# Rebuilding the opening of an expert-mixing stage, with weight tiles of the next stage transferred earlier

## The chip, the cores and the metric

One Trainium2 chip, one core, one launch. The metric is the device time of the whole program in microseconds (us). Each run gives one time; a separate profiled execution gives the trace from which all rows below are taken. PE is the matrix engine (PEld its weight loads), DVE the vector engine, ACT the scalar engine, POOL GpSimd, SP the engine that issues the transfers here.

## The reference, cut to what matters

Eight blocks run one after the other on 1024 tokens of 512 features, each as `x = layernorm(x + block(x))`. The change touches the seams of four of them:

```python
x = _layernorm(x + _L0_attn_ref(x, ...))  # series + SwiGLU (F = 1248)
x = _layernorm(x + _L0_ffn_ref(x, ...))   # mix of 8 low-rank experts
x = _layernorm(x + _L1_attn_ref(x, ...))  # as laid out here: one key, so values only
x = _layernorm(x + _L1_ffn_ref(x, ...))   # SwiGLU, int weights with zeros and scales
...                                       # L2: convolution stack, two low-rank layers
x = _layernorm(x + _L3_attn_ref(x, ...))  # causal attention
x = _layernorm(x + _L3_ffn_ref(x, ...))   # SwiGLU, int weights with one scale each

def _L0_ffn_ref(x, W_org, lora_down, lora_up, lora_keys, Wq):
    base = jnp.einsum('bsi,oi->bso', x, W_org)
    q = jnp.einsum('bi,ki->bk', x.mean(axis=1), Wq)
    scores = jnp.einsum('bk,ek->be', q, lora_keys) / math.sqrt(K)
    coeffs = jax.nn.softmax(scores, axis=-1)
    h = jnp.einsum('bsi,eir->bser', x, lora_down)
    delta = jnp.einsum('be,bser,ero->bso', coeffs, h, lora_up)
    return base + delta
```

The expert mix is one weight matrix for all tokens, because the batch is one and the coefficients come from the mean token: `w_eff = W_org + down @ (coeff * up)`. So nothing of this block can start before the last token of the block ahead is normalised, summed, and taken through the query, the scores, the softmax and the scaled `up` matrix.

## The kernel before, in words

Tokens lie twice in SBUF: `x_tok` (tokens on partitions, 8 tiles of 128) and `x_feat` (features on partitions, 4 chunks of 128). Every engine has its own program; they meet through semaphores, and each stage is a `Block`, at whose end all engines wait for each other. There is no planner in the stages that the change touches; the order within an engine is the order of the code, except in the attention stage, where a list of events gives it.

A `Tail` ends each block of the model, tile by tile: DVE adds the product to `x_tok` (L95), takes statistics (L101, L102), ACT takes the root (L111), DVE normalises (L104, L105), PE transposes (L147), ACT copies the transposed tile to `x_feat` (L119). Where `start` is given, the copy goes straight into the next SwiGLU's input instead, split into a high part by ACT and a low part by DVE (`dve_low`, L125).

The first block is `swiglu` with a series added (`gradient_ffn`). In its second half, for each of eight token tiles, PE makes the series products (L820, from `series_part`, which ACT and DVE split at L799 and L811) and the down products (L577), and the tail follows one tile behind.

The expert stage is `lora_then_single_key`. Its opening: SP issues the transfers of the query matrix, the keys, `up` and `down`, then of `wo` (eight groups through three buffers, a buffer being free once `paired`), of `W_org` and of `wv`. DVE and ACT sum `x_feat` over the tokens (L1101, L1064), PE makes the query (L1019) and the scores (L1023), DVE and ACT the softmax (L1109 to L1114), ACT scales one half of `up`'s partitions and DVE the other, four instructions each (L1072, L1118). Then PE makes `delta`, 16 matrix products of four bytes a value (L1029, two records each), DVE adds `W_org` (L1137), and PE goes through the eight token tiles (L938). Merging `wv` and `wo` into `w_values` (L1042) and a second pass through the tiles (L938 again) follow. In that second pass the first two weight tiles of the next SwiGLU are already dequantised by DVE (`dequantise`: L325 takes the zeros off, L328 and L330 multiply by the scales), split by ACT (L364) and DVE (L369), and multiplied (L382).

The next stage, the SwiGLU with zeros and scales, has 14 weight tiles through two slots of `stage`, and one buffer each for zeros (`z_int`) and scales (`s_all`). SP loads tile f when tile f-2 is split (`w_lo`) and its zeros and scales when those of tile f-1 are used (`zs_used`). PE makes 48 products per tile (L560), ACT the silu (L614, L619), DVE the multiplication (L708, L715). POOL computes a table of rotations beside it (`Rotation.pool`), with instructions that get longer level by level.

## Time and profile before

| | us |
|---|---|
| runs | 1326.65, 1332.54, 1592.5 (median 1332.54) |
| profiled execution, time | 1336.08 |
| its span in the trace | 1334.4 |
| PE busy | 1244.7 (93% of the span) |
| DVE busy | 713.8 (53%) |
| ACT busy | 433.5 (32%) |
| POOL busy | 160.9 (12%) |
| mean granted PE clock | 0.971 of full |

The profiled execution's time exceeds its span by 1.7 us, which lie around the program. Engines work at the same time, so their busy times don't add up; what counts is the chain of waits, and on a kernel with PE at 93% that is first of all where PE stands still.

### The profile page before, as it was taken

The page shows a single profiled execution, that of the slowest core. Times are in us where ns is not written, and L with a number is a line of the kernel's source. Part 1 is how long each engine was busy: PE and PEld are TensorE (multiplying, and loading weights), DVE is VectorE, ACT ScalarE, POOL GpSimd, SP SyncE. Part 2 cuts the span into 40 slices and gives each one's busy share as a digit, 9 for nine tenths or more (in the row PEclk, how much of TensorE's full clock was granted, in tenths as well). Part 3 has the DMA queues.
Part 4 walks back from the last instruction along what each step waited for, and adds up shares of the span by engine and source line. Part 5 has one row for each costly group of instructions (what it writes and reads, how often), then busy time and mean ns, then how long its engine had stood idle before and what let it go on. Part 6 is the DMA issues. An engine that isn't in the chain of part 4 may idle for free. (4 is left out here: it accounts for less than half of the span.)

```text
span 1334.4 us, 14306 instructions
## 1 busy us (share of the span) xinstructions
PE 1244.7 (93%) x5325; PEld 845.4 (63%) x5336; DVE 713.8 (53%) x1191; ACT 433.5 (32%) x743; POOL 160.9 (12%) x214
## 2 busy tenths in 40 slices
PE   7899999699988999999887988899999998999998
PEld 4788688344477788788654435455555543688886
DVE  4421534368737655553434749787776744344344
ACT  2121422211111113321233221265666567222221
POOL 0000000000057300101111250000011124000000
PEclk9899999799999999998898989999999999999999
DMA  8110000643044562103000010000000000122001
GB/s 338 32 48 16 0 1 0 250 169 141 1 166 178 195 229 83 45 0 133 2 0 1 0 48 1 1 1 2 2 1 1 3 3 0 48 95 71 0 25 40
DMA packets 18264, 79.06 MB, mean 59 GB/s; under 512 B 3104, under 2 KB 3872, under 8 KB 16032
## 3 DMA queue, kind: packets, MB, share of 16 engines
q1 hardware_dynamic: 18208, 78.32, 16.1%
q8 instruction: 34, 0.56, 0.2%
q14 instruction: 22, 0.18, 0.0%
HBM read 75.95 MB, written 2.10 MB: 58 GB/s over the span
## 5 line engine op out<-in xcount | busy, mean ns | idle before, releaser
L2264 DVE TENSOR_REDUCE mqa_top<-psum 128x1 f32<-128x512 f32 (+3 forms) x304 | 186.3, 656 | 48.1 <-PE psum L2056 25.7
L2171 ACT ACTIVATE mqa_prob<-psum 128x512 f32<-128x512 f32 x288 | 156.5, 603 | 81.2 <-PE psum L2086 77.6
L560 PE MATMUL psum<-L_ffn_x,L_ffn_w_up 128*128 128x512 f32 x624 | 146.3, 396 | 8.7 <-DVE L_ffn_hidden L708 4.8
L560 PEld LDWEIGHTS psum<-L_ffn_x,L_ffn_w_up 128*128 128x128 f32 x624 | 118.9, 191 | 36.1 <-DVE L_ffn_hidden L708 6.3
L560 PE MATMUL psum<-L_attn_x,L_attn_w_up 128*128 128x512 f32 x456 | 106.2, 395 | 3.9 <-DVE L_attn_hidden L708 3.9
L560 PEld LDWEIGHTS psum<-L_attn_x,L_attn_w_up 128*128 128x128 f32 x456 | 87.2, 192 | 22.6 <-issue 4.3
L2086 PE MATMUL psum<-mqa_stack_back,mqa_keys 100*128 100x512 f32 x208 | 95.5, 459 | 0.9 <-DVE mqa_stack_front L2255 0.9
L111 ACT ACTIVATE ln_std<-ln_mean_var,eps 128x1 f32<-128x1 f32 x56 | 16.5, 295 | 196.8 <-DVE ln_mean_var L102 196.8
L2099 PE MATMUL psum<-mqa_prob,mqa_v 128*32 128x512 f32 x576 | 77.8, 605 | 0.0
L1986 POOL TENSOR_SCALAR_AFFINE_SELECT mqa_prob<-mqa_prob 128x512 f32<-128x512 f32 x64 | 41.7, 671 | 257.7 <-ACT mqa_prob L2171 257.5
L2056 PE MATMUL psum<-mqa_keys,mqa_stack_back 96*128 96x512 f32 (+1 forms) x160 | 68.2, 449 | 4.8 <-DVE mqa_stack_back L2255 2.3
L2086 PEld LDWEIGHTS psum<-mqa_stack_back,mqa_keys 100*128 100x128 f32 x208 | 39.6, 190 | 49.5 <-ACT mqa_prob L2171 42.8
L607 ACT CAST L_ffn_w_up<-L_ffn_stage 128x1024 fp32r<-128x1024 f32 x21 | 22.1, 1050 | 132.3 <-DVE L_ffn_stage L328 92.3
L459 DVE TENSOR_TENSOR L_ffn_part_h<-L_ffn_hidden,L_ffn_part_h 128x896 fp32r<-128x896 f32 (+2 forms) x32 | 31.6, 992 | 60.3 <-ACT L_ffn_part_h L456 60.3
L560 PE MATMUL psum<-L_ffn_x_front,L_ffn_w_up 128*128 128x512 f32 x264 | 63.1, 395 | 0.3 <-PEq L1942 0.3
L577 PE MATMUL psum<-L_ffn_wd,L_ffn_part_h 128*128 128x512 f32 x264 | 61.8, 395 | 0.0
L577 PE MATMUL psum<-L_attn_wd,L_attn_part_h 128*128 128x512 f32 x240 | 58.8, 397 | 0.0
L95 DVE TENSOR_TENSOR x_tok<-x_tok,psum 128x512 f32<-128x512 f32 x56 | 38.2, 682 | 37.9 <-PE psum L938 17.2
L560 PEld LDWEIGHTS psum<-L_ffn_x_front,L_ffn_w_up 128*128 128x128 f32 x264 | 49.4, 187 | 12.7 <-issue 0.7
L577 PEld LDWEIGHTS psum<-L_ffn_wd,L_ffn_part_h 128*128 128x128 f32 x264 | 49.5, 188 | 12.0
L708 DVE TENSOR_TENSOR L_attn_hidden<-L_attn_gate,psum 128x512 f32 (+1 forms) x20 | 13.8, 688 | 76.7 <-PE psum L560 75.9
L577 PEld LDWEIGHTS psum<-L_attn_wd,L_attn_part_h 128*128 128x128 f32 x240 | 44.6, 188 | 10.1 <-issue 1.0
(298 smaller groups left out, 2050.0 us busy)
## 6 DMA issues: line engine op xcount, KB each, us to landing
L_ffn_stage<-in_L_w SPq DMA_DIRECT2D x25, 768.0 KB, 6.3
L_ffn_z_int<-in_L_z SPq DMA_DIRECT2D x14, 768.0 KB, 4.4
L_ffn_s_all<-in_L_s SPq DMA_DIRECT2D x14, 768.0 KB, 6.1
lora_wo<-in_L_wo SPq DMA_DIRECT2D x8, 1024.0 KB, 9.5
L_attn_stage<-in_L_w SPq DMA_DIRECT2D x10, 512.0 KB, 3.5
L_attn_w_down<-in_L_down SPq DMA_DIRECT2D x1, 2560.0 KB, 24.7
x_feat<-in_x_feat SPq DMA_DIRECT2D x2, 1024.0 KB, 7.1
x_tok<-in_x_tok SPq DMA_DIRECT2D x1, 2048.0 KB, 19.1
```

What stands on the lines that cost most here:

```text
L95: nc.vector.tensor_tensor(row, row, self.out_bank[t % 2][:, :], ALU.add).then_inc(self.out_taken, 1)
L111: nc.scalar.activation(c.std[:, t:t + 1], c.mean_var[:, t, 1:2], ACT.Sqrt, bias=c.eps[:, 0:1]).then_inc(self.std_ready, 1)
L459: nc.vector.tensor_tensor(part_h[:, g, 1, 0:n, :], src, part_h[:, g, 0, 0:n, :].bitcast(F32), ALU.subtract).then_inc(h_lo, 1)
L560: ins = nc.tensor.matmul(bank[place][:, :], w_up[:, slot, w_part, at:at + P], x_half[half][:, x_part, k, :], start=k == 0 and n == 0, stop ...
L577: ins = nc.tensor.matmul(tail.out_bank[t % 2][:, :], part_h[:, g, h_part, f - groups[g].start, :], wd(w_part, f), start=f == 0 and n == 0 ...
L607: nc.scalar.copy(w_up[:, slot, 0, :], stage[:, slot, 0:up_width]).then_inc(w_hi, 1)
L1986: nc.gpsimd.affine_select(out=tile, in_=tile, compare_op=ALU.is_ge, fill=0.0, base=0, pattern=[[0, 4], [1, P]], channel_multiplier=-1).the ...
L2056: ins = nc.tensor.matmul(out[:, 0:width], held[0:SPLIT, heads[0] // 2, tile], keys[0:SPLIT, heads[0] % 2, lo:lo + width], start=True, stop ...
L2086: ins = nc.tensor.matmul(score_bank[n % 3], keys[0:SHIFTED, head, cols(kt)], held[0:SHIFTED, 4 * g:4 * g + 4, tile], start=True, stop=True)
L2099: nc.tensor.matmul(value_bank[row:row + 32, :], v[:, kt, :], prob[:, n % PROBS, :], start=kt == 0, stop=final).then_inc(value_done, 1)
L2171: nc.scalar.activation(prob[:, n % PROBS, :], score_bank[n % 3], ACT.Exp, scale=SCALE)\
L2264: nc.vector.tensor_reduce(top[:, i % 2, 2 if lo == qt * P else lo // HALF, heads[0]:heads[-1] + 1], max_bank[n % 3][:, 0:len(heads) * widt ...
```

## The change

In the first stage, DVE sums each token tile of `x_feat` as soon as it is there (`add_tokens`, tiles 0 to 6, one column of `token_sum` each), and SP issues the transfers of the query matrix, the keys, `up` and `down` behind the last low part of the series. The last token tile is neither transposed nor copied in that stage. In the expert stage PE takes the last tile's sums by products of `x_tok` with a column of ones, makes the query from the eight columns of sums, and only then transposes the last tile. DVE adds the eight query columns; the division by the number of tokens goes into the instruction that widens the query. The coefficients are laid out so that `up` is scaled with all 128 partitions: two of its four pieces by DVE, two by ACT, and PE starts each `delta` product when its piece is there. SP issues `W_org` first. The first weight tiles of the next SwiGLU wait for `delta`; behind them SP also issues tiles 2 and 3 (and the zeros and scales of tiles 1 and 2) in the expert stage, as `load_next`, and likewise at the end of the attention stage for the last SwiGLU. The dequantisation of weight tile 1 is put behind two token tiles instead of one. There is no product whose result is not read. Below, memory layout, names of semaphores and unchanged lines are left out.

```diff
-def each_tile(eng, tiles, body):
+def each_tile(eng, tiles, body, begun=0):
...
+    if not begun:
+        body(0, 0, True)
+        body(1, 1, True)
+    if tiles >= 4 + begun:
+        with eng.Fori(1 + begun // 2, tiles // 2) as i:
...
             nc.gpsimd.memset(c.eps[:, :], EPS)
+            nc.gpsimd.memset(c.one[:, :], 1.0)
...
-    def dequantise(self, dve, f, slot, first):
+    def dequantise(self, dve, f, slot, first, pieces=(0, 1)):
...
+            if 0 in pieces:
+                dve.wait_ge(front.zs_loaded, 32 * f + 32)
+                nc.vector.tensor_tensor(front.stage[:, slot, :], front.raw[:, slot, :], front.z_int[:, :],
+                                        ALU.subtract).then_inc(front.centred, 1)
+            if 1 not in pieces:
+                return
             dve.wait_ge(front.centred, f + 1)
...
+    def load_next(self, sp):
+        front, base = self.front, self.c.ffn_base
+        for slot in range(2):
+            if front.zeros is not None:
+                sp.wait_ge(front.zs_used, slot + 1)
+                front.load_zeros_scales(sp, slot + 1)
+            sp.wait_ge(self.w_lo, base["w_lo"] + slot + 1)
+            front.load_tile(sp, 2 + slot, slot)
...
-                each_tile(sp, tiles, load)
+                if start is not None and zeros is not None:
+                    sp.wait_ge(front.zs_used, 3)
+                    front.load_zeros_scales(sp, 3)
+                each_tile(sp, tiles, load, 0 if start is None else 2)
...
+                if expert is not None:
+                    expert.load(sp, a, extra_split)
...
-                tail.pe(pe, NT - 1)
+                if expert is None:
+                    tail.pe(pe, NT - 1)
...
+                    if expert is not None and t == NT - 1:
+                        tail.act_copy(act, t - 1)
+                        tail.act_std(act, t)
+                        break
...
+                    if expert is not None and t == NT - 1:
+                        expert.add_tokens(dve, tail, t - 1)
                     tail.dve(dve, t)
                     if t + 2 < NT:
                         split_h(dve, t + 2, 0, 1)
+                    if expert is not None and 1 <= t < NT - 1:
+                        expert.add_tokens(dve, tail, t - 1)
...
+class ExpertEntry:
...
+    def load(self, sp, a, series):
+        sp.wait_ge(series.low, NT - series.FIRST)
+        sp.dma_start(self.wq[:, :, :], a["L0_wq"]).then_inc(self.q_loaded, 16)
+        sp.dma_start(self.keys[:, :], a["L0_keys"]).then_inc(self.q_loaded, 16)
+        sp.dma_start(self.up[:, :, :], a["L0_up"]).then_inc(self.w_loaded, 16)
+        sp.dma_start(self.down[:, :, :], a["L0_lora_down"]).then_inc(self.w_loaded, 16)
+
+    def add_tokens(self, dve, tail, t):
+        c = self.c
+        dve.wait_ge(tail.feat_ready, tail.base + t + 1)
+        c.nc.vector.tensor_reduce(c.token_sum[:, :, t], c.x_feat[:, :, t * P:(t + 1) * P], AX.X, ALU.add)
...
             def _(sp):
-                sp.dma_start(wq[:, :, :], a["L0_wq"]).then_inc(q_loaded, 16)
-                sp.dma_start(keys[:, :], a["L0_keys"]).then_inc(q_loaded, 16)
-                sp.dma_start(up[:, :, :], a["L0_up"]).then_inc(w_loaded, 16)
-                sp.dma_start(down[:, :, :], a["L0_lora_down"]).then_inc(w_loaded, 16)
+                sp.dma_start(w_org[:, :, :], a["L0_org"]).then_inc(org_loaded, 16)
...
-                    if g == 1:
-                        sp.dma_start(w_org[:, :, :], a["L0_org"]).then_inc(org_loaded, 16)
...
+                sp.wait_ge(delta_ready, KC)
                 front.load_first(sp)
                 if start is not None:
-                    sp.wait_ge(front.zs_used, 1)
-                    front.load_zeros_scales(sp, 1)
+                    start.load_next(sp)
...
             def _(pe):
+                x_last = c.x_tok[:, NT - 1, :]
+                pe.wait_ge(entry.tail.normed, entry.tail.base + NT)
+                for k in range(KC):
+                    ins = nc.tensor.matmul(c.bank[0][:, k:k + 1], x_last[:, k * P:(k + 1) * P], c.one[:, 0:1],
+                                           start=True, stop=True)
+                ins.then_inc(by_pe, 1)
                 pe.wait_ge(q_loaded, 32)
-                pe.wait_ge(mean_ready, 1)
+                pe.wait_ge(by_dve, SUM)
                 for k in range(KC):
-                    ins = nc.tensor.matmul(c.bank[0][:, 0:1], wq[:, k, :], mean[:, k:k + 1],
+                    ins = nc.tensor.matmul(c.bank[1][:, 0:NT], wq[:, k, :], c.token_sum[:, k, :],
                                            start=k == 0, stop=k == KC - 1)
-                ins.then_inc(q_ready, 1)
-                pe.wait_ge(wide_ready, 1)
-                nc.tensor.matmul(c.bank[1][:, 0:E], q_wide[:, :], keys[:, :], start=True, stop=True)\
-                    .then_inc(scores_ready, 1)
+                ins.then_inc(by_pe, 1)
+                entry.tail.pe(pe, NT - 1)
+                pe.wait_ge(by_dve, WIDE)
+                nc.tensor.matmul(c.bank[2][:, 0:E], q_wide[:, :], keys[:, :], start=True, stop=True)\
+                    .then_inc(by_pe, 1)
                 pe.wait_ge(w_loaded, 32)
-                pe.wait_ge(coeff_ready, 2)
                 for i in range(KC):
                     for r in range(RC):
+                        if i == 0:
+                            if r < RC // 2:
+                                pe.wait_ge(by_dve, UP + r + 1)
+                            else:
+                                pe.wait_ge(up_by_act, r - RC // 2 + 1)
                         ins = nc.tensor.matmul(c.bank[i][:, :], down[:, r, i * P:(i + 1) * P], up_c[:, r, :],
...
+                pe.wait_ge(entry.tail.feat_ready, entry.tail.base + NT)
                 pe.wait_ge(eff_ready, KC)
...
             def _(act):
-                for k in range(2, KC):
-                    nc.scalar.activation(wide_sum[:, k - 2, :], c.x_feat[:, k, :], ACT.Copy,
-                                         accum_out=mean[:, k:k + 1]).then_inc(mean_by_act, 1)
...
-                for r in range(RC):
-                    ins = nc.scalar.activation(up_c[0:R, r, :], up[0:R, r, :], ACT.Copy,
-                                               scale=coeff[0:R, 2 * r:2 * r + 1])
-                ins.then_inc(coeff_ready, 1)
+                for r in range(RC // 2, RC):
+                    nc.scalar.activation(up_c[:, r, :], up[:, r, :], ACT.Copy, scale=coeff[:, r:r + 1])\
+                        .then_inc(up_by_act, 1)
+                entry.tail.act_copy(act, NT - 1)
...
-                then(nc.vector.tensor_reduce(mean[:, 0:2], c.x_feat[:, 0:2, :], AX.X, ALU.add))
-                dve.wait_ge(mean_by_act, 2)
-                nc.vector.tensor_scalar(mean[:, :], mean[:, :], 1.0 / TOK, None, ALU.mult).then_inc(mean_ready, 1)
-                dve.wait_ge(q_ready, 1)
-                then(nc.vector.tensor_copy(q[:, :], c.bank[0][:, 0:1]))
+                dve.wait_ge(by_pe, LAST_ADDED)
+                nc.vector.tensor_copy(c.token_sum[:, :, NT - 1], c.bank[0][:, 0:KC]).then_inc(by_dve, 1)
+                dve.wait_ge(by_pe, Q)
+                then(nc.vector.tensor_reduce(q[:, :], c.bank[1][:, 0:NT], AX.X, ALU.add))
...
-                then(nc.vector.tensor_scalar(coeff[:, :], e[:, :], inv[:, 0:1], None, ALU.mult))
+                by_half = e[:, :].rearrange("p (r h) -> p h r", h=2)
+                for h in range(2):
+                    rows = slice(h * R, (h + 1) * R)
+                    then(nc.vector.tensor_scalar(coeff[rows, :], by_half[rows, h, :], inv[rows, 0:1], None, ALU.mult))
...
-                for r in range(RC):
-                    ins = nc.vector.tensor_scalar(up_c[R:P, r, :], up[R:P, r, :], coeff[R:P, 2 * r + 1:2 * r + 2],
-                                                  None, ALU.mult)
-                ins.then_inc(coeff_ready, 1)
+                for r in range(RC // 2):
+                    nc.vector.tensor_scalar(up_c[:, r, :], up[:, r, :], coeff[:, r:r + 1], None, ALU.mult)\
+                        .then_inc(by_dve, 1)
...
-                    if start is not None and t == 1:
-                        start.room.dequantise(dve, 1, 1, True)
+                    if start is not None and t in (1, 2):
+                        start.room.dequantise(dve, 1, 1, True, (t - 1,))
...
+                start.load_next(sp)
```

## Rows read from the trace of the kernel before

**Rows 1.** Who PE waited for, whole span: us in total, times, longest.

```profile
PE psum L1029 <- ACT lora_up_c L1072: 5.8, 1, 5.8
...
PE psum L560 <- DVE L_ffn_hidden L708: 4.8, 2, 3.8
...
PE psum L560 <- DVE L_ffn_w_up L701: 3.5, 1, 3.5
```

**Rows 2.** Timeline of the expert opening: start, duration, engine, line, out<-in, count [idle before].

```profile
242.50 0.55 DVE L105 TENSOR_SCALAR x_tok<-x_tok,ln_mean_var,ln_rstd 128x512 f32<-128x512 f32 x1
...
243.98 0.58 ACT L119 COPY x_feat<-psum 128x512 f32<-128x512 f32 x1 [1.24 <-PE psum L147]
...
245.04 2.29 DVE L1101 TENSOR_REDUCE lora_mean<-x_feat 128x2 f32<-128x2048 f32 x1 [1.99 <-PEq L471]
...
247.91 1.86 PE L1019 MATMUL psum<-lora_mean,lora_wq 128*128 128x1 f32 x8 [3.96 <-DMA lora_keys<-in_L_keys]
...
252.06 0.23 DVE L1114 TENSOR_SCALAR lora_coeff<-lora_e,lora_inv 128x8 f32<-128x8 f32 x1
...
254.05 2.56 ACT L1072 ACTIVATE lora_up_c<-lora_up,lora_coeff 64x512 f32<-64x512 f32 x4 [2.42 <-DMA lora_down<-in_L_lora_down]
...
254.12 1.70 DVE L1118 TENSOR_SCALAR lora_up_c<-lora_up,lora_coeff 64x512 f32<-64x512 f32 x4 [1.84 <-DMA lora_down<-in_L_lora_down]
...
256.75 15.84 PE L1029 MATMUL psum<-lora_up_c,lora_down 128*128 128x512 f32 x32 [5.82 <-ACT lora_up_c L1072]
```

**Rows 3.** Stretches of the opening: busy per engine, granted PE clock, DMA share, GB/s.

```profile
251.00:256.50 5.50, 0.00 (x0) 0.00 (x0) 2.54 (x9) 2.71 (x5) 0.00 (x0) 0.50 1.01 419
...
260.00:262.00 2.00, 2.00 (x5) 0.87 (x4) 0.00 (x0) 0.00 (x0) 0.00 (x0) 0.87 1.04 438
```

**Rows 4.** Timeline of the first stage's end, tiles 6 and 7.

```profile
226.33 1.09 DVE L811 TENSOR_TENSOR series_part<-series_terms,series_part 128x896 fp32r<-128x896 f32 x1 [0.50 <-ACT series_part L799]
...
227.93 2.50 PE L820 MATMUL psum<-L_attn_w_split,series_part 128*128 128x512 f32 x10
...
240.31 0.69 DVE L95 TENSOR_TENSOR x_tok<-x_tok,psum 128x512 f32<-128x512 f32 x1 [7.94 <-PE psum L577]
```

**Rows 5.** The page's costliest groups: a reduction of 512 columns, busy and mean ns.

```profile
L2264 DVE TENSOR_REDUCE mqa_top<-psum 128x1 f32<-128x512 f32 (+3 forms) x304 | 186.3, 656 | 48.1 <-PE psum L2056 25.7
```

**Rows 6.** Timeline of the second pass of the expert stage.

```profile
343.31 1.75 DVE L325 TENSOR_TENSOR L_ffn_stage<-L_ffn_stage,L_ffn_z_int 128x1536 f32<-128x1536 int32 x1
...
349.63 0.66 PE L147 MATMUL psum<-ident,x_tok 128*128 128x128 f32 x4 [1.87 <-DVE x_tok L105]
```

**Rows 7.** Timeline of the SwiGLU with zeros and scales, first tiles.

```profile
377.52 11.16 PE L560 MATMUL psum<-L_ffn_x,L_ffn_w_up 128*128 128x512 f32 x48 [0.33 <-PEq L988]
...
383.35 0.69 DVE L715 TENSOR_TENSOR L_ffn_hidden<-L_ffn_gate,psum 128x512 f32<-128x512 f32 x1 [4.48 <-PE psum L560]
...
386.54 1.76 DVE L325 TENSOR_TENSOR L_ffn_stage<-L_ffn_stage,L_ffn_z_int 128x1536 f32<-128x1536 int32 x1 [2.51 <-DMA L_ffn_s_all<-in_L_s]
...
388.33 1.22 DVE L328 TENSOR_TENSOR L_ffn_stage<-L_ffn_stage,L_ffn_s_all 128x1024 f32<-128x1024 f32 x1
...
392.23 23.80 PE L560 MATMUL psum<-L_ffn_x,L_ffn_w_up 128*128 128x512 f32 x96 [3.55 <-DVE L_ffn_w_up L701]
...
409.04 3.45 POOL L1311 TENSOR_TENSOR x_feat<-x_feat,rot_turn 128x1024 f32<-128x1024 f32 x1
...
410.77 2.80 DVE L328 TENSOR_TENSOR L_ffn_stage<-L_ffn_stage,L_ffn_s_all 128x1024 f32<-128x1024 f32 x1
...
419.81 45.74 PE L560 MATMUL psum<-L_ffn_x,L_ffn_w_up 128*128 128x512 f32 x192 [3.78 <-DVE L_ffn_hidden L708]
```

**Rows 8.** A stretch of the same stage, columns as in Rows 3.

```profile
394.00:395.00 1.00, 1.00 (x3) 0.77 (x3) 0.00 (x0) 0.00 (x0) 0.92 (x2) 0.50 0.98 363
```

**Rows 9.** Transfers on the page: issues, KB each, median us to landing.

```profile
L_ffn_s_all<-in_L_s SPq DMA_DIRECT2D x14, 768.0 KB, 6.1
```

**Rows 10.** Timeline at the start of the last SwiGLU.

```profile
1156.59 17.03 PE L560 MATMUL psum<-L_ffn_x_front,L_ffn_w_up 128*128 128x512 f32 x72 [0.33 <-PEq L1942]
```

More of the change, by code:

```diff
@@ L401, in swiglu @@
            extra_dve=None, extra_pe=None, extra_act=None, extra_split=None, table=None, ahead=None, a=None,
-           start=None):
+           start=None, expert=None):
     nc = c.nc
@@ L493, in load @@
                         front.load_tile(sp, f, slot)
-                    if zeros is not None and not (first and (slot == 0 or start is not None)):
+                    if zeros is not None and not (first and slot == 0):
                         sp.wait_ge(front.zs_used, f)
@@ L680, in _ @@
                         tail.act_copy(act, t - 1)
-                if not tail.last:
+                if not tail.last and expert is None:
                     tail.act_copy(act, NT - 1)
@@ L940, in product_tiles, with __init__, sb, lora_then_single_key @@
     ins.then_inc(tail.out_ready, 1)
-def lora_then_single_key(c, a, front, start):
-    nc = c.nc
+class ExpertEntry:
     E, R, K = 8, 64, P
     RC = E * R // P
+    def __init__(self, c, below):
+        self.c, self.tail = c, None
+        with ExitStack() as own:
+            def sb(n, shape):
+                return c.sb(f"lora_{n}", shape, F32, own)
+            sb("below_entry", [P, below // 4])
+            self.up, self.down = sb("up", [P, self.RC, DIM]), sb("down", [P, self.RC, DIM])
+            self.wq, self.keys = sb("wq", [P, KC, self.K]), sb("keys", [P, self.E])
+        self.w_loaded, self.q_loaded = c.sem("lora_w_loaded"), c.sem("lora_q_loaded")
+    def load(self, sp, a, series):
[8 more added lines that the diff above has]
+        c.nc.vector.tensor_reduce(c.token_sum[:, :, t], c.x_feat[:, :, t * P:(t + 1) * P], AX.X, ALU.add)
+def lora_then_single_key(c, a, front, start, entry):
+    nc = c.nc
+    E, R, K, RC = entry.E, entry.R, entry.K, entry.RC
     KV, PER, SLOTS = 8, 4, 3
@@ L2334, in build @@
         setup(c)
-        gradient_ffn(c, a)
+        entry = ExpertEntry(c, 16992)
+        gradient_ffn(c, a, entry)
         c.rot = Rotation(c)
```

51 lines of the change are left out of this document (25 added, 26 removed).

## The prediction

> **What bounds the kernel now.** I read the page first: PE is busy for 93% of the span, so a gain is either PE time taken out or a PE wait that goes. No big product is taken out here, so I went to the list of who PE waited for [rows 1]. Three of its entries lie where the change works: 5.8 us ahead of the `delta` products, and 3.5 and 4.8 us in the SwiGLU with zeros and scales. Then I read those places in order of time. In the opening [rows 2], the last token tile is normalised at 243.05 and `delta` starts at 256.75: 13.7 us in which PE makes 1.86 us of query products and little else. The reader should see two different causes there: up to the coefficients (252.29) a chain of small steps, and from there to 254.05 a transfer, the one of `down`; the DMA engines are full in that stretch, at 419 GB/s [rows 3]. The granted clock is 0.50 there, the 1.2 GHz level, and between 260 and 262 it is 0.87 on average, so it went back to 2.4 GHz after about 0.5 us of that stretch, at 260.5 [rows 3].
>
> In the SwiGLU [rows 7], tiles 0 and 1 keep PE busy from 377.52 to 388.68, then it waits 3.55 us. DVE starts tile 2's dequantisation at 386.54, after 2.51 us of waiting for the scales, because these transfers are issued only when the stage begins. After that gap the clock falls for a while (0.50 at 394 to 395) [rows 8]. A second wait, of 3.78 us, ends at 419.81.
>
> **The change, part by part.** The opening. What is left on the path, step by step: the first stage now ends with the normalisation at 243.05 instead of the copy that ends at 244.56. Before, DVE's first instruction came 0.48 us behind that end [rows 2], so the stage begins at 243.53. The sums of the last tile are four products with one column; the four query products with one column are the nearest row, 1.86 us, and I take it for them: 245.39. DVE copies four columns and passes on: a small DVE instruction is 0.23 us, with the handovers 0.3: 245.7. The query now has eight columns for one; the price stays 1.86: 247.55. From the end of the query to the end of the coefficients it was 249.77 to 252.29, 2.52 us. Into this come a second coefficient instruction (0.23) and the last tile's transposes, which stand on PE between query and scores: four take 0.66 us [rows 6], up to twice that at the low clock, while DVE makes the widened query; I take 0.3 of them as exposed. That gives 250.6. `up` and `down` are transferred long before (next part), so the 1.8 us wait goes. One piece of `up` is 1.70 / 4 = 0.43 us on DVE (ACT's is 2.56 / 4 = 0.64 and begins beside it), and PE needs only the first: `delta` starts at 251.1 instead of 256.75, 5.65 us earlier. With all transposes exposed and each handover doubled it would be 4.6. I take `delta` itself at the 15.84 us it has now, low clock at its head included.
>
> What is next late: the next step needs `W_org`, which now goes first instead of behind seven other transfers, and the copy of the last tile, which ACT makes after its two pieces, some 15 us ahead of need. The first `wo` group is now behind one 1 MB transfer instead of four, and DVE has the whole of `delta` for its first sum. From here to the second pass everything hangs on PE and moves with it.
>
> The first stage. Seven sums of one tile each (512 columns) are put on DVE: five ahead of a low part of the series, one behind tile 6's normalisation, one just ahead of the last tile. A reduction of 512 columns takes 0.66 us [rows 5]; a quarter of the 2048-column one gives 0.57 [rows 2]. DVE idles 0.50 us just ahead of the low part, as shown for the last one, which ends at 227.42, while PE's first product of it starts at 227.93 [rows 4]. The sum goes into that idle time and makes the low part up to 0.16 us late, which the gap behind it covers: nothing. If that cover is gone, 5 times 0.16 is 0.8 us lost. The other two fall into idle time, the last into DVE's 7.94 us ahead of 240.31 [rows 4]: nothing. SP's new wait, for the last low part of the series, has nothing behind it in that stage; that part ends 12.9 us ahead of 240.31, and the 2.4 MB (three matrices of 128 x 512, 128 x 2048 and 128 x 2048 values) at 419 GB/s take 5.6 us. The extra memset at the start is one column: nothing, at most 0.2.
>
> The second pass. DVE's dequantisation of tile 1 in one piece (1.75 us for its first instruction alone, 343.31) makes the next tile late, and PE waits 1.87 us for it [rows 6]. In two pieces, each tile is late by half, and the second piece pushes the next tile's normalisation to 0.2 us ahead of where it is now. I take 0.4 us of gain; the ends are 0 and 1.87.
>
> The early weight tiles. SP's waits in the expert stage (`zs_used`, `w_lo` of tiles 0 and 1) are all met before that stage ends and have nothing queued behind them; the new wait for `delta` is met 20 us before the transfer that it holds back was issued so far. In the SwiGLU, tile 2's dequantisation can then start when DVE is free, after 383.35 + 0.69 = 384.04, 2.5 us earlier than 386.54. PE's first gap shrinks from 3.55 to 1.05 us. The nearest gap of that size is the 1.87 us at 349.63 [rows 6], so the clock may stay up; the low stretch costs 23.80 - 2 x 11.16 = 1.5 us now. But only 2.5 us are certain, as tile 3 has a chain of its own: its zeros and scales wait for the use of tile 2's, which moves by the same 2.5 us, land 6.1 us [rows 9] after the issue, and DVE needs several us for them. So the 1.5 us of clock become waiting time, unless the chain gets shorter too. It does, in part: the later a dequantisation falls, the longer are the POOL instructions beside it. One scaling takes 1.22 us at 388.33 and 2.80 us at 410.77, with a POOL instruction lying from 409.04 to 412.49 across its start [rows 7]. From the earlier start, about one such collision of 2.80 - 1.22 = 1.6 us is missed before PE's second wait. I take 1.5, together 4.0 us. The ends: 2.5 less one collision more, 1.0; and 2.5 + 1.5 + (45.74 - 4 x 11.16 = 1.1 of the second low stretch) + the last wait of 1.0 (4.8 - 3.8 [rows 1]) = 6.1.
>
> The Trainium skill, page "SBUF — State Buffer", section "Who interferes with whom", has a rule for such collisions: a DVE instruction with two inputs in SBUF and a GpSimd instruction that reads SBUF exclude each other for a whole instruction, and the one that began first keeps the ports. The trace agrees: DVE's 2.80 us end 1.08 us behind POOL's, nearly its own 1.22. By that rule the two streams would alternate, which is the first rival below, and the sum would be 8.55 instead of 10.05.
>
> At the last SwiGLU, PE starts at 1156.59 and runs 17.03 us for 72 products without a wait [rows 10], so the early transfers there are worth nothing, and cost nothing: SP has no other work behind them.
>
> Sum: 5.65 + 0.4 + 4.0 = 10.05 us. Against the profiled execution's own time: 1336.08 - 10.05 = 1326.0. That execution lies 3.5 us above the median shown; against the median it is 1332.54 - 10.05 = 1322.5. I say 1324, the middle.
>
> **The rivals** (times by the profiled execution). First, DVE and POOL take turns all the way between PE's two waits, so that each DVE instruction pays for one POOL instruction whatever its start, and no collision is missed: 2.5 in the SwiGLU instead of 4.0, gain 8.55, time 1327.5. For it: the one collision shown ends with POOL's instruction. Against it: POOL's instructions are shorter earlier on.
>
> Then, the SwiGLU gives nothing: the second wait re-forms at its old place in the stage. For it: DVE and POOL are dense there [rows 7]. Against it: POOL runs from the stage's start without looking at tile 2. Gain 6.05, time 1330.
>
> Third, more than I forecast: the small products now stand close together, the clock rises ahead of `delta`, and the SwiGLU's gaps vanish. Low until 260.5 costs 3.75 x 0.5 = 1.9 us now. Against it: 1.86 us of such products before did not raise it. Gain 5.65 + 1.9 + 1.87 + 6.1 = 15.5, time 1320.6.
>
> Fourth, slower: the opening keeps PE busy too thinly, nothing fills it, and the clock stays at 1.2 GHz through `delta` and on. `delta` would take 2 x 13.9 = 27.9 us, 12 more: 1338, and more for each token tile behind it. It decides from about 20 us of low clock beyond what there is. Against it: the same `delta`, after 5.8 us of no products at all, got its clock back within 3.8 us [rows 3].
>
> Fifth, the transfers of `up` and `down` come no earlier in effect, and 1.8 us of waiting remain in the opening: 1327.8.
>
> **How the numbers follow.** Forecast 0.50, first rival 0.18, second 0.10, third 0.14, fourth 0.04, fifth 0.04. The range: from the fastest run less the largest gain, 1326.65 - 15.5 = 1311, to the profiled execution less the smallest, 4.6 + 0 + 1.0 - 0.8 - 0.2 = 4.6, so 1332. Two per cent, about what a measurement here can tell from no change, is 26.6 us; no gain above reaches it, and only the fourth rival's far end does, on the other side. Faster 0.03, same 0.95, slower 0.02.
>
> **What would show it.** `delta` starting about 8 us behind the last normalisation, with no transfer named ahead of it; its 15.84 us unchanged; the first SwiGLU wait near 1 us and the clock at 1.00 behind it; the second wait smaller than 3.78; the first stage's last product still ending near 240.3; the same start of work at the last SwiGLU, less about 10 us. Wrong would make it: a clock that stays low behind the opening, sums on DVE that hold up the series, or waits in the SwiGLU that only change their place.

## The result and the profile after

The changed kernel takes 1319.82 us in the median of 4 runs (1315.81 to 1325.35), the kernel before 1335.51 us beside it; the ratio is 0.9891 [0.986, 0.9922], so 14.5 us less. That is 1.1 per cent, below the two per cent that the prediction took for what a measurement can tell from no change, and yet clear of no change by its interval. Three executions are far longer than all others, 1592.5 us of before here and below 3135.62 of the change and 2077.21 of the opening alone; the medians hold them (without its one, that of before is 1332.54), the ratios and means do not. The profiled execution of after took 1316.08 us with a span of 1314.4; before it was 1336.08 and 1334.4, so these two traces lie 20 us apart. Both are more than the forecast's 10.05 us, and the question of the study is where the rest comes from.

The opening after, in order of time (start, duration, engine, line, out<-in, count, idle time before and its releaser), which answers to [rows 2]:

```profile
240.41 0.55 DVE L105 TENSOR_SCALAR x_tok<-x_tok,ln_mean_var,ln_rstd 128x512 f32<-128x512 f32 x1
...
241.28 1.84 PE L1075 MATMUL psum<-eps,x_tok 128*128 128x1 f32 x8 [3.10 <-PEq L487]
...
243.47 1.84 PE L1081 MATMUL psum<-token_sum,lora_wq 128*128 128x8 f32 x8 [0.35 <-DVE token_sum L1167]
...
245.16 1.09 PE L147 MATMUL psum<-ident,x_tok 128*128 128x128 f32 x4
...
247.61 0.48 DVE L1182 TENSOR_SCALAR lora_coeff<-lora_e,lora_inv 64x4 f32<-64x4 f32 x2
248.13 0.88 DVE L1186 TENSOR_SCALAR lora_up_c<-lora_up,lora_coeff 128x512 f32<-128x512 f32 x2
...
248.76 2.90 PE L1096 MATMUL psum<-lora_up_c,lora_down 128*128 128x512 f32 x3 [2.28 <-DVE lora_up_c L1186]
```

From the end of the last normalisation (240.41 + 0.55 = 240.96) to `delta` it is 7.80 us; it was 13.70. No transfer stands ahead of anything here any more: PE's wait of 5.82 us in [rows 2] has become 2.28 us, for DVE's first piece of `up`, at 248.13. The transposes of the last tile (L147) stand between the query products and the scores.

The clock there, by stretches of the same trace (span, then busy us and count of PE, PEld, DVE, ACT and POOL, granted clock, DMA share, GB/s), to set beside [rows 3]:

```profile
246.00:248.00 2.00, 0.49 (x4) 0.39 (x2) 1.00 (x6) 0.27 (x1) 0.00 (x0) 0.50 1.00 422
...
252.00:254.00 2.00, 2.00 (x3) 0.67 (x2) 0.00 (x0) 0.00 (x0) 0.00 (x0) 0.50 1.02 410
254.00:256.00 2.00, 2.00 (x6) 0.99 (x5) 0.68 (x2) 0.00 (x0) 0.00 (x0) 0.91 1.08 455
```

The clock is at its 1.2 GHz level (0.50) ahead of `delta` and goes back about 5.6 us behind its start at 248.76, later than the 3.8 us of before. So `delta` did not get cheaper by the denser products. The later return belongs to this execution: in the two other traces of the change, taken below, `delta` starts at 249.43 and 249.58, and the stretch from 252 to 254 has 0.80 and 0.87, so the clock goes back 3.4 and 2.9 us behind the start.

The second pass of the expert stage, PE in order of time, which answers to [rows 6]:

```profile
345.70 0.66 PE L147 MATMUL psum<-ident,x_tok 128*128 128x128 f32 x4 [0.89 <-DVE x_tok L105]
...
349.63 0.60 PE L147 MATMUL psum<-ident,x_tok 128*128 128x128 f32 x4
```

One wait of 0.89 us is left of the 1.87. The next fence is the SwiGLU with zeros and scales, PE's rows, to set beside [rows 7]:

```profile
369.69 11.14 PE L581 MATMUL psum<-L_ffn_x,L_ffn_w_up 128*128 128x512 f32 x48 [0.32 <-PEq L1049]
381.59 11.15 PE L581 MATMUL psum<-L_ffn_x,L_ffn_w_up 128*128 128x512 f32 x48 [0.76 <-DVE L_ffn_w_up L727]
393.43 11.18 PE L581 MATMUL psum<-L_ffn_x,L_ffn_w_up 128*128 128x512 f32 x48 [0.69 <-DVE L_ffn_hidden L734]
407.58 12.79 PE L581 MATMUL psum<-L_ffn_x,L_ffn_w_up 128*128 128x512 f32 x48 [2.97 <-DVE L_ffn_hidden L734]
421.87 33.51 PE L581 MATMUL psum<-L_ffn_x,L_ffn_w_up 128*128 128x512 f32 x144 [1.50 <-DVE L_ffn_hidden L734]
```

The first wait is 0.76 us, was 3.55, and the 11.15 and 11.18 us behind it show no low clock. But a wait of 2.97 us comes two tiles later, with 12.79 us for 48 products behind it instead of 11.15. What DVE and GpSimd did in that stretch:

```profile
400.44 1.95 DVE L335 TENSOR_TENSOR L_ffn_stage<-L_ffn_stage,L_ffn_s_all 128x1024 f32<-128x1024 f32 x1
...
404.02 2.91 DVE L727 TENSOR_TENSOR L_ffn_w_up<-L_ffn_stage,L_ffn_w_up 128x1024 fp32r<-128x1024 f32 x1
```

```profile
401.39 2.16 POOL L1384 TENSOR_TENSOR x_feat<-x_feat 128x512 f32<-128x512 f32 x1
403.62 2.23 POOL L1378 TENSOR_TENSOR x_feat<-x_feat,rot_turn 128x1024 f32<-128x1024 f32 x1
405.93 2.75 POOL L1379 TENSOR_TENSOR wave<-wave,rot_turn 128x1024 f32<-128x1024 f32 x1
```

DVE's instruction at 404.02 takes 2.91 us where the same one takes 1.23 undisturbed: GpSimd's began at 403.62 and ends at 405.85, and DVE's ends 1.08 us behind that, at 406.93. GpSimd's next began at 405.93 and ends 1.75 us behind DVE's. They go in turns. Added up, the four instructions that DVE makes for a weight tile (L330, L335, L337 and L727; before L325, L328, L330 and L701) took, in us, with the table last (an experiment below, in which GpSimd is silent there) for comparison:

| weight tile | before | after | GpSimd silent |
|---|---|---|---|
| 2 | 5.22 | 4.94 | 4.94 |
| 3 | 7.11 | 6.09 | 4.91 |
| 4 | 10.30 | 9.02 | 4.89 |
| 5 | 7.82 | 10.75 | 4.91 |
| sum | 30.45 | 30.80 | 19.65 |

In the kernel before, PE's second wait stands ahead of tile 4. Up to that tile DVE now needs 2.6 us less; tile 5 takes 2.9 more, and the sum is nearly the same.

### By stages

Where the rest of the 20 us lies is found by cutting each trace at starts of rows: the last product of the series, the first of `delta`, the first with `W_eff` (first pass), the first with `w_values` (second pass), the first GpSimd row of the table (SwiGLU), the transfers of `conv_centre` and `two_low` (from here the convolution stage, as it is called below), the scales of the third expert block, `mqa_stack_back`, the first row of the last SwiGLU. For after the first is 248.76 - 230.46 = 18.3. In us:

| trace | series to delta | delta to first pass | second pass to SwiGLU | SwiGLU stage | convolution stage | rest |
|---|---|---|---|---|---|---|
| before | 24.2 | 16.6 | 44.6 | 161.5 | 159.5 | 928.0 |
| before again | 24.6 | 16.4 | 44.6 | 161.5 | 156.0 | 926.3 |
| opening alone | 18.1 | 16.4 | 44.5 | 161.4 | 159.4 | 926.0 |
| early tiles alone | 24.7 | 16.3 | 43.8 | 159.1 | 158.6 | 930.2 |
| after | 18.3 | 17.6 | 43.8 | 159.2 | 151.0 | 924.5 |
| after again | 18.0 | 16.5 | 43.8 | 159.1 | 162.3 | 929.1 |
| after, third | 18.2 | 16.2 | 43.8 | 159.1 | 162.3 | 926.4 |
| table later | 17.9 | 16.6 | 43.8 | 155.5 | 156.8 | 925.8 |
| six unread products | 17.9 | 14.7 | 43.8 | 159.1 | 156.8 | 928.1 |
| one piece | 18.3 | 16.2 | 44.6 | 160.1 | 156.6 | 928.7 |
| table later, four unread | 16.5 | 17.0 | 43.8 | 155.5 | 163.2 | 925.9 |
| one unread product | 17.8 | 16.6 | 43.8 | 159.1 | 156.8 | 925.7 |

The rest is the span less the five. (The table last, below, has another order there and is left out.) In the first, third and fourth column every kernel has its own value, within 0.4 us (the first is 24.2 to 24.7 with the old opening, 17.9 to 18.3 with the rebuilt one). The convolution stage and the rest go with the execution: the same code takes 151.0 and 162.3 us there.

### The profile page after: what moved, and what is told of

It is laid out like the page before. It is cut to its first block and busy times, and to the rows that moved or that the text cites. A ratio compares the mean times of both kernels' runs of the same rounds, so it can differ in the third digit from the quotient of the medians.

```text
span 1314.4 us, 14299 instructions
## 1 busy us (share of the span) xinstructions
PE 1234.0 (94%) x5333; PEld 837.5 (64%) x5344; DVE 716.9 (55%) x1196; ACT 430.1 (33%) x737; POOL 163.2 (12%) x215
## 3 DMA queue, kind: packets, MB, share of 16 engines
q1 hardware_dynamic: 18208, 78.32, 16.5%
## 5 line engine op out<-in xcount | busy, mean ns | idle before, releaser
L111 ACT ACTIVATE ln_std<-ln_mean_var,eps 128x1 f32<-128x1 f32 x56 | 16.5, 294 | 189.0 <-DVE ln_mean_var L102 189.0
L95 DVE TENSOR_TENSOR x_tok<-x_tok,psum 128x512 f32<-128x512 f32 x56 | 38.2, 682 | 30.5 <-PE psum L970 16.4
L598 PEld LDWEIGHTS psum<-L_attn_wd,L_attn_part_h 128*128 128x128 f32 x240 | 44.6, 188 | 10.1 <-issue 1.0
```

Source lines behind the costliest of these rows:

```text
L95: nc.vector.tensor_tensor(row, row, self.out_bank[t % 2][:, :], ALU.add).then_inc(self.out_taken, 1)
L111: nc.scalar.activation(c.std[:, t:t + 1], c.mean_var[:, t, 1:2], ACT.Sqrt, bias=c.eps[:, 0:1]).then_inc(self.std_ready, 1)
L598: ins = nc.tensor.matmul(tail.out_bank[t % 2][:, :], part_h[:, g, h_part, f - groups[g].start, :], wd(w_part, f), start=f == 0 and n == 0 ...
```

## The experiments

Theory A for the whole: the change's own places give about 10 us, and what the first result shows beyond that is a stage elsewhere that varies from execution to execution. Theory B, the rival: the change itself gives 14 to 20 us. Where a run asks about a single place, its expectation says what the theories are there.

**The kernel before, against itself,** with no edit.

> The kernel before against itself. Theory A (the change's own places give about 8 us, and the rest of the 14.5 us between the runs so far is where the clock happened to fall): ratio 1.000, and the times of its stages away from the change, the convolution stack above all, differ by up to 8 us from one profiled execution to the next. Theory B (the change moves later stages to a better place): ratio 1.000 too, but its convolution stack takes the same time as in the first trace of it, within 1 us.

1331.11 us in 12 runs beside 1335.69 in 30, ratio 0.9992 [0.9967, 1.0018]. The trace of this one is 5.0 us shorter than that of before (1329.4 to 1334.4), with the same code: 3.5 us of it are the convolution stage. B allowed 1 us there, so A holds in this run.

**The changed kernel again,** with no edit.

> The changed kernel again. Theory A: ratio to before 0.993 to 0.995 (8 to 10 us), and a convolution stack whose time is drawn from the same spread as that of the kernel before. Theory B: 0.988 to 0.990 (13 to 16 us), with a convolution stack that is again some 8 us shorter than before's 159 us.

1325.61 us in 7 runs, ratio 0.9923 [0.9896, 0.9949], 10.3 us. The span of its trace is 1328.8 us, 14.4 more than that of the first, and 11.3 of these lie in the convolution stage. Two stretches of that stage in the first trace of after, which begins it at 607.9 us:

```profile
608.00:628.00 20.00, 17.20 (x101) 13.59 (x102) 10.19 (x14) 5.85 (x10) 9.27 (x7) 1.00 0.64 224
...
708.00:728.00 20.00, 18.82 (x53) 8.69 (x52) 14.16 (x31) 4.43 (x11) 5.06 (x4) 0.83 0.01 2
```

And the same ones in the second trace, which begins it at 607.5:

```profile
608.00:628.00 20.00, 18.64 (x76) 15.79 (x77) 7.80 (x11) 3.88 (x6) 6.02 (x6) 0.66 0.63 224
708.00:728.00 20.00, 15.24 (x46) 7.78 (x45) 8.24 (x18) 6.23 (x11) 4.52 (x4) 0.66 0.00 1
```

The granted clock is 1.00 and 0.83 in one and 0.66 twice in the other, for the same code, and PE has 101 or 76 records in the first 20 us. The 151.0 us are the shortest convolution stage of all thirteen traces, and the next is 156.0, so the first trace of after was a lucky one. By this stage B falls: it had a stage again some 8 us shorter than that of before. By the ratio alone the two can't be told apart: 0.9923 lies just below the 0.993 to 0.995 of A, and the interval reaches into the 0.988 to 0.990 of B.

**The opening alone.** The change without the early weight tiles and without the split dequantisation:

```diff
-                    start.load_next(sp)
+                    sp.wait_ge(front.zs_used, 1)
+                    front.load_zeros_scales(sp, 1)
...
-                each_tile(sp, tiles, load, 0 if start is None else 2)
+                each_tile(sp, tiles, load)
...
-                    if start is not None and t in (1, 2):
-                        start.room.dequantise(dve, 1, 1, True, (t - 1,))
+                    if start is not None and t == 1:
+                        start.room.dequantise(dve, 1, 1, True)
```

> The rebuilt opening alone, weight tiles as before. By the forecast's terms: 5.65 us for the opening, ratio 0.9958; by what the trace of the changed kernel shows (5.9 for the start of delta, 0.9 given back by delta itself) 5 us, ratio 0.9963. The waits of 3.5 and 3.8 us in the SwiGLU are back. Rival: the opening is worth less than 2 us in the whole because the second pass waits for something else, ratio over 0.9985.

1332.11 us, ratio 0.9974 [0.9951, 0.9998], so 3.5 us. By stages it has the whole gain of the opening (18.1 us for 24.2) and nothing else. The rival (less than 2 us, a ratio over 0.9985) lies inside the interval of the ratio; it is the stages that exclude it. In the SwiGLU the old waits come back, here PE's rows of it:

```profile
384.45 23.81 PE L578 MATMUL psum<-L_ffn_x,L_ffn_w_up 128*128 128x512 f32 x96 [3.58 <-DVE L_ffn_w_up L724]
411.90 18.46 PE L578 MATMUL psum<-L_ffn_x,L_ffn_w_up 128*128 128x512 f32 x73 [3.64 <-DVE L_ffn_hidden L731]
```

**The early tiles alone.** The kernel before with `load_next`, the loop that begins behind them, and the split dequantisation (the lines above, the other way round, and `start.load_next(sp)` in the attention block).

> The early weight tiles and the dequantisation in two pieces alone, old opening. By the forecast: 4.0 + 0.4 us, ratio 0.9967. By the first rival (DVE and POOL take turns): 2.5 + 0.4 us, ratio 0.9978, and the wait that shrinks from 3.5 to about 1 us comes back as several of 1 to 3 us in the next tiles. By the second rival: nothing, 0.9997.

1333.18 us, ratio 0.998 [0.9955, 1.0005], 2.7 us. By stages: the second pass 43.8 for 44.6, the SwiGLU 159.1 for 161.5, the opening unchanged at 24.7. The interval of the ratio holds the forecast and both rivals of this run; the stages, 0.8 + 2.4 us, are the price of the first rival. Of the several waits of 1 to 3 us that this rival foresaw, one of 2.96 us is there and the others are below 1. The two halves make 3.5 + 2.7 = 6.2 us by the ratios, below the 10.3 of the whole but within their intervals; by stages they make 6.1 and 3.2 and nothing is lost between them.

**One piece.** The change with tile 1 dequantised in one piece, as the last four lines of the diff of the opening alone.

> The changed kernel with the dequantisation of weight tile 1 in one piece again. The second pass (first product with w_values to the next stage) goes back from 43.8 to 44.6 us, and the PE wait of 1.9 us for a normalisation is back; the forecast's term of 0.4 would make it 44.2.

One execution, 1326.24 us. The second pass is back at 44.6 us, as expected, so the split is what gives the 0.8. The SwiGLU has 160.1, with a wait of 3.08 us where the change has 1.50; why the split helps there too is not shown.

**The table later.** GpSimd builds a table during the SwiGLU, and from level 7 on its instructions have 512 to 2048 columns. Here they are held until tile 2 is done, and then come three, two or one at a time, each group behind one more tile:

```diff
             n, ops = 1 << level, 0
+            if level == 7:
+                after_tile(pool, 2)
+                tile = 3
```

> The changed kernel with POOL's three longest levels of the rotation table held back: the first of them waits for weight tile 2, and each later group for one more tile, so that POOL's long instructions fall into DVE's waits for scales. Theory A (turns between DVE and POOL re-form the waits behind tile 2): of the waits of 0.7, 3.0, 1.5 and 1.0 us at least the 3.0 and 1.5 go, the low clock behind the 3.0 us gap too, and the stage from its first POOL instruction to the convolution's first transfer falls from 159.1 to 153 to 156 us; ratio to before 0.988 to 0.990. Rival (the waits come from the single buffer of zeros and scales, whatever POOL does): the stage stays within 1 us of 159.1.

1318.64 us in 6 runs beside 1334.28, ratio 0.9875 [0.9841, 0.9909]. PE's and DVE's rows of the same place:

```profile
392.94 33.37 PE L581 MATMUL psum<-L_ffn_x,L_ffn_w_up 128*128 128x512 f32 x144 [0.59 <-DVE L_ffn_hidden L734]
```

```profile
399.74 1.23 DVE L335 TENSOR_TENSOR L_ffn_stage<-L_ffn_stage,L_ffn_s_all 128x1024 f32<-128x1024 f32 x1
...
402.17 1.23 DVE L727 TENSOR_TENSOR L_ffn_w_up<-L_ffn_stage,L_ffn_w_up 128x1024 fp32r<-128x1024 f32 x1 [0.60 <-ACT L_ffn_w_up L629]
```

The scaling takes 1.23 us, not 1.95, PE runs 144 products without a wait where it had waits of 2.97 and 1.50, and the stage takes 155.5 us for 159.1, inside the 153 to 156 of A; the ratio lies just below the 0.988 expected.

**The table last.** The same, but from level 5 on and held until tile 12:

```diff
+            if level == 5:
+                after_tile(pool, 12)
+                tile = 4
```

> The changed kernel with POOL's table from its sixth level on put behind weight tile 12, as a measure and not as a candidate, since the stage's end then waits for the table. Theory A: between tiles 2 and 12 DVE's instructions keep their undisturbed times (1.75, 1.23, 0.68, 1.23 us) and PE has one wait of 0.8 us ahead of tile 2 and none over 0.3 us behind it. Rival (single buffer of zeros and scales): waits of 1 us and more remain between tiles 3 and 6.

One execution, 1344.25 us, and both sides of the price. First PE behind tile 1:

```profile
382.01 88.31 PE L581 MATMUL psum<-L_ffn_x,L_ffn_w_up 128*128 128x512 f32 x388 [0.76 <-DVE L_ffn_w_up L727]
```

With GpSimd silent PE has no further wait, and DVE's scalings have their 1.22 or 1.23 us until GpSimd begins again at 503.00. That the second wait is made by GpSimd's instructions, and not by the single buffer of zeros and scales, is thereby shown. At the end PE waits 17.8 us once; the list of who it waited for, then ACT and DVE just ahead:

```profile
PE psum L598 <- DVE L_ffn_part_h L475: 17.8, 1, 17.8
```

```profile
549.59 1.78 ACT L472 CAST L_ffn_part_h<-L_ffn_hidden 128x896 fp32r<-128x896 f32 x2 [31.30 <-POOL scan_start L1393]
550.57 2.10 DVE L475 TENSOR_TENSOR L_ffn_part_h<-L_ffn_hidden,L_ffn_part_h 128x896 fp32r<-128x896 f32 x2 [18.41 <-ACT L_ffn_part_h L472]
```

The list names DVE, but DVE waited for ACT, and ACT for GpSimd's last instruction of the table: this wait is no collision, the end of the stage waits for the whole table, as was foreseen.

**Six unread products,** to keep the clock up ahead of `delta`: four of 512 columns at the end of the first stage and two ahead of `delta`. Nobody reads their result.

```diff
                 if expert is None:
                     tail.pe(pe, NT - 1)
+                else:
+                    for _ in range(4):
+                        nc.tensor.matmul(c.bank[3][:, :], c.ident[:, :], c.x_feat[:, 0, 0:HALF], start=True, stop=True)
...
+                for _ in range(2):
+                    nc.tensor.matmul(c.bank[3][:, :], c.ident[:, :], c.x_feat[:, 0, 0:HALF], start=True, stop=True)
                 pe.wait_ge(w_loaded, 32)
```

> The changed kernel with six products whose result is not read, four behind the last product of the first stage and two ahead of delta. If thin PE work is what lets the clock fall in the opening: granted clock 1.00 from the first stage to delta, the two groups of small products take about half of 1.84 us each, delta with its tail takes 14 instead of 16.5 us; 3 to 5 us below the changed kernel, ratio to before 0.989. If six are too few to hold the clock or lie on the path: no more than 1 us either way.

1320.42 us in 6 runs, ratio 0.9886 [0.9849, 0.9923]. The clock, to set beside the stretches of after:

```profile
246.00:248.00 2.00, 2.00 (x4) 0.72 (x3) 1.60 (x6) 0.99 (x3) 0.00 (x0) 0.55 1.03 421
248.00:250.00 2.00, 2.00 (x6) 0.90 (x5) 0.87 (x2) 1.98 (x3) 0.00 (x0) 1.00 1.02 430
```

And PE:

```profile
243.33 1.03 PE L1084 MATMUL psum<-token_sum,lora_wq 128*128 128x8 f32 x8 [0.35 <-DVE token_sum L1172]
...
245.38 3.16 PE L1092 MATMUL psum<-x_feat,ident 128*128 128x512 f32 x4
248.38 1.88 PE L1101 MATMUL psum<-lora_up_c,lora_down 128*128 128x512 f32 x4
```

The small products run at the 2.4 GHz level, 1.03 us instead of 1.84, but the clock falls between 244 and 246 all the same, so the two late ones take 3.16 us and end where `delta` begins. The four early ones cost something too: the stage's first product starts 241.95 - 230.50 = 11.45 us behind the last of the series, in after 10.82. What the small products won is spent on both, and series to `delta` is 17.9 as without. `delta` then runs at full clock and the next stage takes 14.7 us for 16.2 to 17.6. Both stages together take 32.6 us, the change 34.5 to 35.9: about 2 us in all, where 3 to 5 were expected.

**The table later, with three early and one late unread product; one late one alone; the change once more.** Edits as above with other counts, beside the same executions of before.

> The change with GpSimd's second batch of table levels put behind tile 2 of the SwiGLU, three unread products at the end of the first stage and one ahead of the delta products. If the gains of the two edits are what their own stages showed (Theory A: each place counts by itself), the SwiGLU stage stays at 155 to 156 us against 159.1, the opening stage at 17.5 to 18.3, the delta stage falls to 14.5 to 15.5 against 16.5 to 17.5, and the whole is 5 to 6 us below the change: ratio to before 0.985 to 0.989 if the change stands at 0.989 to 0.992 in the same call. If what is won by the clock is given back by the later stages (Theory B), the stages show the same but the ratio is the change's.

> The change with one unread product ahead of the delta products and nothing else. It falls into TensorE's idle 1.6 us between 246.8 and 248.4 at a granted clock of 0.50, where one such product takes about 1.6 us, so the opening stage should stay at 18.0 to 18.4. If the clock rises by the work that TensorE has just done, it rises some 1.5 us sooner and the delta products save about 0.8 us: delta stage 15.5 to 16. If only a long unbroken run at the delta products themselves raises it, the delta stage is 16.3 to 17.5 as in the change. The whole is within 0.3% of the change by either.

> The change itself a third time, beside the two variants. Theory A (the change's own places give 9.5 to 10 us): ratio to before 0.990 to 0.994, opening stage 18.0 to 18.4, second pass to SwiGLU 43.8, SwiGLU stage 159.1; the stage of the convolution and the two adapters anywhere from 151 to 162 us. Theory B (14 to 20 us, as in the first result): 0.986 to 0.989 and the convolution stage near 151 us.

Beside 1335.48 us: 1317.93 in 6 runs, ratio 0.9894 [0.9851, 0.9937]; 1320.62 in 10, 0.9906 [0.9877, 0.9934]; 1323.32 in 10, 0.9907 [0.9875, 0.9938]. The first missed its `delta`: 17.0 us, expected 14.5 to 15.5, and its ratio lies just above the expected 0.989, in an interval too wide to tell it from the change. The SwiGLU's 155.5 us held. The stretches of that run:

```profile
246.00:248.00 2.00, 1.61 (x3) 0.50 (x2) 1.50 (x5) 1.21 (x2) 0.00 (x0) 0.50 1.00 419
248.00:250.00 2.00, 2.00 (x3) 0.67 (x2) 0.95 (x1) 1.88 (x3) 0.00 (x0) 0.50 1.05 442
250.00:252.00 2.00, 2.00 (x4) 0.90 (x3) 0.97 (x2) 0.00 (x0) 0.00 (x0) 0.55 0.97 410
```

The opening is shorter (16.5 us, expected 17.5 to 18.3), since the late product ends before the coefficients do, but `delta` starts at 247.37 and its first 4 us or so are at 0.50. Opening and `delta` together are 33.5 us, with six products 32.6, with the change 34.5 to 35.9. One late product alone gives nothing: 34.5 us together, and a `delta` stage of 16.6, the second of its two expectations. The third run of the change again agrees with A by its ratio and its stages; its convolution stage took 162.3 us, as in the second. B's ratio, 0.986 to 0.989, is not excluded by the interval; B's convolution stage is.

## Why the prediction was right, and where it was not

**The opening** (5.65 us) came out at 13.70 - 7.80 = 5.90 between normalisation and `delta`, and 6.1 by the stages in the kernel that has it alone. Step by step: from the start of the sums to the end of the query it was 245.31 - 241.28 = 4.03 us, foreseen 4.02; from there to the coefficients 248.09 - 245.31 = 2.78, foreseen 3.05. The eight narrow products cost 1.84 us each time, as the nearest row said. The fifth rival, transfers that come no earlier, is out.

**The first stage** (nothing) was right. The sums of a tile fall into gaps; two of DVE's rows:

```profile
230.17 0.68 DVE L1001 TENSOR_REDUCE token_sum<-x_feat 128x4 f32<-128x512 f32 x1
...
235.39 0.69 DVE L1001 TENSOR_REDUCE token_sum<-x_feat 128x4 f32<-128x512 f32 x1 [4.54 <-ACT x_feat L119]
```

From the first product of the series to the last it is 65.6 us in all thirteen traces, with the sums and without them.

**`delta`** (unchanged) was right on the average: 16.2 to 17.6 us to the first pass with the change, 16.4 to 16.6 before. In the first trace the clock came back later than before, in the two others sooner. The third rival's condition, a clock that rises ahead of `delta`, did not occur; it took unread products. Nor did the fourth's: no trace shows a clock that stays down.

**The second pass** was taken as 0.4 and gave 0.8 (44.6 to 43.8); the wait fell by 1.87 - 0.89 = 0.98.

**The SwiGLU** is the mis-sized term: 4.0 forecast, 161.5 - 159.1 = 2.4 measured. The first wait went as foreseen (1.05 forecast, 0.76 shown) and the clock held behind it. What failed is the step that "about one such collision of 2.80 - 1.22 = 1.6 us is missed before PE's second wait": the sum ends at that wait and takes it as nothing that something behind it could give the gain back. Up to there it was even better than forecast. From the stage's first product to tile 4's it was 419.81 - 377.52 = 42.29 us and is 407.58 - 369.69 = 37.89, so 4.4 won. At PE's last wait for `hidden`, first in before, then in after, only 2.4 of it is left (it comes 89.04 and 86.69 us behind the first product):

```profile
466.56 3.70 PE L560 MATMUL psum<-L_ffn_x,L_ffn_w_up 128*128 128x512 f32 x15 [1.01 <-DVE L_ffn_hidden L708]
```

```profile
456.38 3.94 PE L581 MATMUL psum<-L_ffn_x,L_ffn_w_up 128*128 128x512 f32 x16 [1.00 <-DVE L_ffn_hidden L734]
```

The collision that was missed ahead of tile 4 comes back at tile 5, whose dequantisation now meets GpSimd's instructions of 1024 columns (10.75 us for 7.82 in the table above), and over tiles 2 to 5 the turns cost the same sum. As waits and clock: those for `w_up` and `hidden` fell from 8.3 us [rows 1] to 0.8 + 6.2 = 7.0, by the list of who PE waited for, and the low clock's cost from 1.5 + 1.1 to 12.79 - 11.15 = 1.6, so 1.3 + 1.0 = 2.3. How the two share it differs between executions: in the second trace of the change tile 4's products take 14.07 us and the wait behind them is 0.22, and the stage takes 159.1 all the same. The price is the first rival's 2.5, and so is the mechanism over tiles 2 to 5: DVE and GpSimd take turns and nothing is saved by an earlier start. The Trainium skill, page "SBUF — State Buffer", section "Who interferes with whom", has the rule that the prediction set beside it, whole instructions that exclude each other; the rows at 403.62 and 404.02 agree, and the table later and last show it by their 1.23 us.

**The last SwiGLU** (nothing) was right; PE's row there still begins without a wait for weights, and from it to the end of the span it is 177.8 us in before and after:

```profile
1136.58 17.04 PE L581 MATMUL psum<-L_ffn_x_front,L_ffn_w_up 128*128 128x512 f32 x72 [0.33 <-PEq L2009]
```

**The sum.** 5.9 + 0.8 + 2.4, and 0.3 between the SwiGLU and the convolution stage (79.5 to 79.1 or 79.2), is 9.4 us by this trace; forecast 10.05. With the `delta` stage counted too, the three traces of the change lie 8.4, 9.8 and 10.0 us below that of before. The SwiGLU gave 1.6 us less than forecast; the opening, the second pass and those 0.3 us, of which the forecast has nothing, gave about 1 us more. That the sum comes so near is in that part luck. The repeated ratios, 0.9923 and 0.9907, are 10.3 and 12.4 us. The forecast time of 1324 lies among the three medians, 1319.82, 1325.61 and 1323.32.

**What stays open.** Over all runs the mean is 1322.4 us in 20 executions of the change (standard error 1.0) and 1334.8 in 74 of before (0.5). That is 12.4 us, give or take 2.2: perhaps 2 to 4 us more than the stages account for. They would lie in the convolution stage and the others that vary, and whether the changed start makes their short times likelier, these runs don't say: the change's three traces there are 151.0, 162.3 and 162.3 us, those of before 159.5 and 156.0. The shortest executions of the two kernels, 1315.52 and 1324.99 us, lie 9.5 us apart, about what the stages give.

A kernel that is better by its stages is at hand: with the table later, the SwiGLU gives 3.6 us more, in both kernels that have it (one of them with four unread products besides). Their 12 executions have a mean of 1318.7 us, 3.7 below the change, which is about what the interval of such a mean can tell.

## What to carry to other kernels

When a transfer is made earlier, follow the work that it frees past the wait that it shortens, and ask which engine will then run beside which: here the work that it freed met GpSimd's long instructions, and holding those back behind the next tile gave more than the earlier transfer had. When a result is larger than its mechanism, cut the traces into stages and run both kernels again before adding to the theory: a stage moved by 11 us between two executions of the same code. Sum the stages that the change can reach, and judge it by those.

## What the hardware showed that was not expected

The convolution stage takes 151.0 to 163.2 us with the same instructions, and the mean granted clock over the stage puts all thirteen traces in order:

| convolution stage, us | mean granted clock | traces |
|---|---|---|
| 151.0 | 0.95 | after |
| 156.0 | 0.91 | before again |
| 156.6 to 156.9 | 0.90 | table later, six unread products, one piece, one unread product, table last |
| 158.6 to 159.5 | 0.89 | before, opening alone, early tiles alone |
| 162.3 to 163.2 | 0.86 | after again, after third, table later with four unread |

The times come in few groups and not all over the range, and one kernel is found in several of them. The first 20 us alone don't decide: two traces with 1.00 there, as in after, took 156.6 and 156.8 us. What puts an execution into its group is not shown. Over whole executions of the change the time follows the mean granted clock: 1315.5 us at 0.984, 1321.3 at 0.979, 1327.75 at 0.971.

What unread products gave and cost here depended on when they ran. Four early ones and two late ones had the clock at 1.00 from 248 us, at `delta`'s start, but the two late ones, at 0.50, took 3.16 us. One alone, 2.05 us long in a wait that is 2.28 us in after, brought nothing.

DVE's subtraction with an int32 input, 1.76 us undisturbed, took 2.17 to 3.47 us beside GpSimd even with the table later (at 397.54 and 477.15), and 4.49 in the change (at 424.21), where a GpSimd instruction of 2048 columns runs.
